# One-hots compared against a row number in PSUM, a ring of five, and a reordered half in a DLRM tower

## The reference

```python
e = jnp.stack([tbl_0[ids[:, 0]], ..., tbl_26[ids[:, 26]]], axis=1)      # 2048 x 27 x 128
inter = jnp.einsum('bfd,bgd->bfg', e, e)                                # pairs f > g are kept: 351
h = jnp.concatenate([bottom, inter_pairs, bottom], axis=1)              # 607
h = jnp.maximum(h @ W_top1 + b_top1, 0.0)                               # 512
h = jnp.maximum(h @ W_top2 + b_top2, 0.0)                               # 256
y = h @ W_top3                                                          # 1
```

## Time and profile before

| | us |
|---|---|
| median of 3 runs (lowest, highest) | 424.97 (424.09, 425.02) |
| the profiled execution | 425.06 |
| its span, first to last instruction | 423.2 |
| busy: PE / PEld | 354.6 / 330.9 |
| busy: POOL / DVE / ACT | 306.2 / 181.0 / 132.9 |

### The profile page before, as it was taken

The page is one execution under the profiler, slowest core; times in us unless marked ns, Lnnn a source line. Parts: engine busy times, 40 slices in busy tenths (PEclk is TensorE's granted clock), DMA queues, the critical chain, the costliest instruction groups (busy, mean ns, idle before and its releaser), DMA issues.

```text
span 423.2 us, 10159 instructions
## 1 busy us (share of the span) xinstructions
PE 354.6 (84%) x4224; PEld 330.9 (78%) x4224; DVE 181.0 (43%) x292; ACT 132.9 (31%) x251; POOL 306.2 (72%) x288
## 2 busy tenths in 40 slices
PE   0094892998999899998999879988999869999937
PEld 0093882998889898988899768987799858988735
DVE  2375845473337522752276133752167232752000
ACT  2222341124322533144313232153221433144303
POOL 6777647787778777877787777877788777877050
PEclk9996895999999999999999989999899989999979
DMA  8958526235432533253333533253332633223020
GB/s 233 224 149 219 144 72 232 61 99 178 103 99 55 176 97 103 49 175 97 74 84 98 166 68 94 53 176 95 76 82 51 208 72 99 49 53 94 16 50 0
DMA packets 46364, 45.74 MB, mean 108 GB/s; under 512 B 34797, under 2 KB 37416, under 8 KB 45296
## 3 DMA queue, kind: packets, MB, share of 16 engines
q1 hardware_dynamic: 34804, 26.09, 22.9%
q0 software_dynamic: 9024, 17.91, 16.4%
q10 hardware_dynamic: 2492, 1.12, 1.1%
HBM read 39.52 MB, written 5.55 MB: 106 GB/s over the span
## 4 chain that ended last, share of the span: by engine, by line
PE 43%; POOL 30%; issue 10%; DMA 8%; SPq 3%; DVE 3%; ACT 2%; ACTq 1%
POOL emb L282 30%; PE work L310 25%; PE work L378 5%; PE gram L338 5%; PE work L321 4%; DMA emb<-in_tbl,ids_all 3%; SPq L233 2%; DMA stages<-in_tbl 2%; DMA h<-in_W_top 1%; PE work L386 1%; PE work L363 1%; DMA h<-in_tbl 1%; DVE tab_lo L429 1%; PE work L365 1%; PE work L364 1%
## 5 line engine op out<-in xcount | busy, mean ns | idle before, releaser
L282 POOL DMA_INDIRECT emb<-in_tbl,ids_all x272 | 299.7, 1102 | 89.4 <-issue 79.3
L310 PE MATMUL work<-onehot,tab_hi 125*128 125x256 f32 x672 | 167.6, 290 | 29.6 <-DVE onehot L441 28.4
L441 DVE TENSOR_SCALAR onehot<-ids_bc,row_idf 125x1024 fp32r<-125x1024 int32 (+1 forms) x208 | 134.4, 663 | 92.3 <-PE work L310 92.0
L310 PE MATMUL work<-onehot,tab_lo 125*128 125x256 f32 x672 | 166.3, 288 | 0.0
L310 PEld LDWEIGHTS work<-onehot,tab_hi 125*128 125x128 f32 x672 | 132.6, 197 | 30.4 <-issue 23.5
L310 PEld LDWEIGHTS work<-onehot,tab_lo 125*128 125x128 f32 x672 | 132.6, 197 | 0.0
L338 PEld LDWEIGHTS gram<-embT 128*54 128x54 f32 x2048 | 55.4, 132 | 19.8 <-issue 12.7
L513 ACT COPY embT<-work 128x512 f32<-128x512 f32 x40 | 29.9, 813 | 126.9 <-PE work L310 126.9
L338 PE MATMUL gram<-embT 128*54 128x52 f32 x2048 | 59.1, 217 | 11.3 <-ACT embT L413 6.0
L321 PE MATMUL work<-ident,emb 128*128 128x128 f32 x272 | 38.8, 283 | 18.3 <-DMA emb<-in_tbl,ids_all 9.8
L321 PEld LDWEIGHTS work<-ident,emb 128*128 128x128 f32 x272 | 30.4, 144 | 24.1 <-issue 11.7
(11 more groups left out here) (31 smaller groups left out, 130.3 us busy)
## 6 DMA issues: line engine op xcount, KB each, us to landing
ids_bc<-in_sel_ids SPq DMA_DIRECT2D x8, 1280.0 KB
grams<-inter SPq DMA_DIRECT2D x64, 84.5 KB
emb<-in_tbl,ids_all POOLq DMA_INDIRECT x272
stages<-in_tbl SPq DMA_DIRECT2D x5, 448.0 KB
h<-in_tbl SPq DMA_DIRECT2D x3, 448.0 KB
stages<-in_tbl SPq DMA_DIRECT2D x2, 560.0 KB
bot<-in_bottom SPq DMA_DIRECT2D x8, 128.0 KB
packed<-grams SPq DMA_DIRECT2D x46, 4.0 KB
```

What stands on the lines that cost most here:

```text
L282: pool.indirect_dma_start(out=emb[:, t % TILE_SLOTS, f, :], out_offset=None, in_=gather_tables[f], in_offset=bass.IndirectOffsetOnAxis(ap= ...
L310: mm = nc.tensor.matmul(out, part[0:k, CHUNK_AT[f] + c, :], onehot[0:k, at % RING, i * HALF:(i + 1) * HALF], start=(c == 0 and i % 2 == 0 ...
L441: nc.vector.tensor_scalar(onehot[0:k, at % RING, 0:len(four) * HALF], ids_bc[0:k, four[0]:four[-1] + 1, :].rearrange("p i n -> p (i n)"), ...
```

## The change

- `BANKS` 4 to 5 and `RING` 3 to 5. To make room, the two staging buffers become `inter` and a new `misc`, and `packed`, `bot` and `y` are parts of `misc`. SP's first load of `bot` and ACT's weight loads wait for the last table's split.
- The one-hot is a tensor against tensor compare; `row_idf`, broadcast along the columns, moves from SBUF to PSUM.
- The first half works in sets of two features (`TWOS`: five sets, 42 one-hots of 512 columns), each set with its own load of ids. ACT rounds the tables of two sets, then those of set j + 2 behind the copies of set j. Later halves keep `FOURS`.
- The even tile's rows go ahead of the last set; in the first half one group goes behind each set from the second on, the last two behind the last. All of them are copied by ACT.
- `mlp1`'s first chunk goes between the last set and the even tile's products. `round_packed` goes behind all four extracts of the even tile.

```diff
-BANKS = 4
+BANKS = 5
-RING = 3
+RING = 5
...
+    TWOS = [(four[a:a + 2], k, chunks) for four, k, chunks in FOURS for a in range(0, len(four), 2)]
+    SETS = [TWOS] + [FOURS] * (HALVES - 1)
...
+    def rows_behind(h, j):
+
+        if h:
+            return range(NGR) if j == max(0, len(FOURS) - 2) else range(0)
+        return range(j - 1, NGR if j == len(TWOS) - 1 else j) if 0 < j <= NGR else range(0)
...
-        row_idf = sb("row_idf", [P, sum(ROW_IDS)])
+        row_idf = ctx.enter_context(nc.psum_tensor("row_idf", [P, sum(ROW_IDS)], F32))
...
-                if n == 0:
-                    sp.dma_start(ids_bc[:, :, :], sel_ids[0].to_broadcast([P, NSEL, HALF])).then_inc(ids_bc_loaded, 16)
+                if i in SET_START:
+                    j = SET_START.index(i)
+                    two = slice(i, i + len(TWOS[j][0]))
+                    sp.dma_start(ids_bc[:, two, :], sel_ids[0][:, two, :].to_broadcast([P, len(TWOS[j][0]), HALF])).then_inc(ids_bc_first[j], 16)
...
+            sp.wait_ge(table_lo, NSEL)
             sp.dma_start(bot[:, :, :], bottom_v[0]).then_inc(bot_loaded, 16)
...
-                for j in range(len(FOURS)):
+                for j in range(len(SETS[h])):
                     select(h, j)
-                rows(2 * h)
+                    rows(2 * h, rows_behind(h, j))
+                if h:
+                    mlp1(h - 1, X_ORDER[:1])
                 products(2 * h, range(GRAMS))
                 if h:
-                    mlp1(h - 1)
+                    mlp1(h - 1, X_ORDER[1:])
...
-                nc.vector.tensor_scalar(onehot[0:k, at % RING, 0:len(four) * HALF],
+                nc.vector.tensor_tensor(onehot[0:k, at % RING, 0:width],
                                         ids_bc[0:k, four[0]:four[-1] + 1, :].rearrange("p i n -> p (i n)"),
-                                        row_idf[0:k, ROW_AT[chunks] + c:ROW_AT[chunks] + c + 1], None, ALU.is_equal).then_inc(onehot_ready, 1)
+                                        row_idf[0:k, ROW_AT[chunks] + c:ROW_AT[chunks] + c + 1].to_broadcast([k, width]), ALU.is_equal).then_inc(onehot_ready, 1)
...
-                for g in range(1, NGR, 2):
-                    rows_out(dve, nc.vector.tensor_copy, 2 * h, g)
...
+                for j in range(len(SETS[h])):
                     select_out(h, j)
-                for g in range(0, NGR, 2):
-                    rows_out(act, nc.scalar.copy, 2 * h, g)
-                extract(2 * h, 0)
+                    if h == 0:
+                        if j + 2 < len(TWOS):
+                            round_tables(j + 2)
+                        elif j + 2 == len(TWOS):
+                            load_weights()
+                    for g in rows_behind(h, j):
+                        rows_out(act, nc.scalar.copy, 2 * h, g)
+                for u in range(GRAMS):
+                    extract(2 * h, u)
                 if h:
                     round_packed(h - 1)
-                for u in range(1, GRAMS):
-                    extract(2 * h, u)
```

More of the change, by code:

```diff
@@ L78, in dlrm_tower @@
     TABLE_ORDER = [i for four, _, _ in FOURS for i in four]
-    ONEHOTS = [(j, c) for j, (_, _, chunks) in enumerate(FOURS) for c in range(chunks)]
+    TWOS = [(four[a:a + 2], k, chunks) for four, k, chunks in FOURS for a in range(0, len(four), 2)]
+    SETS = [TWOS] + [FOURS] * (HALVES - 1)
+    ONEHOTS = [[(j, c) for j, (_, _, chunks) in enumerate(sets) for c in range(chunks)] for sets in SETS]
+    OH_AT = [sum(len(one) for one in ONEHOTS[:h]) for h in range(HALVES + 1)]
     ROW_IDS = sorted({c for _, _, c in FOURS})
     ROW_AT = {c: sum(x for x in ROW_IDS if x < c) for c in ROW_IDS}
-    NOH = len(ONEHOTS)
     GRAMS = P // QUADS // SPAN
@@ L87, in dlrm_tower @@
     COLS = TWO * NG
+    def rows_behind(h, j):
+        if h:
+            return range(NGR) if j == max(0, len(FOURS) - 2) else range(0)
+        return range(j - 1, NGR if j == len(TWOS) - 1 else j) if 0 < j <= NGR else range(0)
+    assert len(TWOS) - 1 <= NGR
+    SET_START = [four[0] for four, _, _ in TWOS]
     use, fill, used, upto = {}, {}, [0] * BANKS, {}
@@ L105, in dlrm_tower @@
     for h in range(HALVES):
-        for j, (four, _, _) in enumerate(FOURS):
+        for j, (four, _, _) in enumerate(SETS[h]):
             for b in range(-(-len(four) // 2)):
                 take("select", h, j, b)
-        for g in range(NGR):
-            take("rows", 2 * h, g)
+            for g in rows_behind(h, j):
+                take("rows", 2 * h, g)
+        upto["gram", 2 * h] = list(used)
         if h:
@@ L142, in dlrm_tower @@
         inter = sb("inter", [P, COLS, QS])
-        stages = sb("stages", [P, 2 * max(CHUNKS) * D])
-        packed = sb("packed", [P, CH, HALF])
-        bot = sb("bot", [P, HALF // P, D])
+        misc = sb("misc", [P, (CH + 2) * HALF])
         x_hi = sb("x_hi", [P, CH + 1, HALF], F32R)
@@ L313, in select, with rows @@
                     mm.then_inc(onehot_used, 1)
-            def rows(t):
-                for g, features in enumerate(GROUPS):
+            def rows(t, groups):
+                for g in groups:
+                    features = GROUPS[g]
                     pe.wait_ge(gathered[t % TILE_SLOTS][g], (t // TILE_SLOTS + 1) * 16 * len(features))
@@ L324, in products @@
             def products(t, us):
-                for b, n in enumerate(upto["rows", t, NGR - 1]):
+                for b, n in enumerate(upto["gram", t]):
                     pe.wait_ge(freed[b], n)
@@ L348, in bottom_rows, with mlp1 @@
                 last.then_inc(filled, 1)
-            def mlp1(h):
+            def mlp1(h, chunks):
                 if h == 0:
                     pe.wait_ge(w1_split, 3)
-                blocks = [take_bank("mlp1", h, m // 2)[:, m % 2 * HALF:(m % 2 + 1) * HALF] for m in range(M1)]
-                for n, c in enumerate(X_ORDER):
-                    k = X_ROWS[c]
+                if X_ORDER[0] in chunks:
+                    for b in range(2):
+                        take_bank("mlp1", h, b)
+                blocks = [bank("mlp1", h, m // 2)[:, m % 2 * HALF:(m % 2 + 1) * HALF] for m in range(M1)]
+                for c in chunks:
+                    k, n = X_ROWS[c], X_ORDER.index(c)
                     if c == CH:
@@ L404, in _ @@
                 products(2 * h + 1, range(2, GRAMS))
-            mlp1(HALVES - 1)
+            mlp1(HALVES - 1, X_ORDER)
             mlp2(HALVES - 1)
@@ L474, in _ @@
             for h in range(HALVES):
-                for n in range(NOH):
-                    if h == 0 and ONEHOTS[n][1] == 0:
-                        for _ in FOURS[ONEHOTS[n][0]][0]:
+                for n, (j, c) in enumerate(ONEHOTS[h]):
+                    if h == 0 and c == 0:
+                        for _ in TWOS[j][0]:
                             split_table(tables)
@@ L494, in _ @@
         def _(act):
[L495 to L505, removed]
+            def round_tables(j):
+                for i in TWOS[j][0]:
+                    n, rows = TABLE_ORDER.index(i), slice(CHUNK_AT[i], CHUNK_AT[i] + CHUNKS[i])
+                    act.wait_ge(table_staged[n % STAGE], 32 * (n // STAGE + 1))
+                    nc.scalar.copy(tab_hi[0:K, rows, :].rearrange("p c d -> p (c d)"), stage[n % STAGE][0:K, 0:CHUNKS[i] * D]).then_inc(table_hi, 1)
@@ new lines, in load_weights @@
+            def load_weights():
+                act.wait_ge(table_lo, NSEL)
+                act.dma_start(w1_bot[0], w_top1[0:D, :]).then_inc(w1_bot_loaded, 16)
+                act.dma_start(w1_bot[1], w_top1[D + PAIRS:, :]).then_inc(w1_bot_loaded, 16)
+                act.dma_start(w2[:, :, :], w_top2.rearrange("(c p) n -> p c n", p=P)).then_inc(weights_loaded, 16)
+                with nc.allow_non_contiguous_dma(reason="a few hundred elements"):
+                    act.dma_start(w3[:, :], w_top3.rearrange("(c p) one -> p (c one)", p=P)).then_inc(weights_loaded, 16)
+                    act.dma_start(b1[:, :], b_top1.rearrange("(c p) -> p c", p=P)).then_inc(weights_loaded, 16)
+                    act.dma_start(b2[:, :], b_top2.rearrange("(c p) -> p c", p=P)).then_inc(weights_loaded, 16)
@@ L507, in select_out @@
             def select_out(h, j):
-                four, k, chunks = FOURS[j]
-                act.wait_ge(onehot_used, h * NOH + max(x for x, one in enumerate(ONEHOTS) if one[0] == j) + 1)
+                four, k, chunks = SETS[h][j]
+                act.wait_ge(onehot_used, OH_AT[h] + max(x for x, one in enumerate(ONEHOTS[h]) if one[0] == j) + 1)
                 for b in range(-(-len(four) // 2)):
```

38 lines of the change are left out of this document (24 added, 14 removed).

## The result

The changed kernel takes 399.74 us (median of 4 runs, 397.87 to 401.33) for 424.53 of the kernel before beside it: ratio 0.9411, 95% interval 0.9367 to 0.9454. The forecast was 399.5 (390 to 412). The profiled execution took 399.54, its span is 397.7.

A forecast was written before the change was run, and what follows sets the result against it. POOL's gathers, stretched beside DVE's one-hots, were taken to bound the kernel from the fourth half on. 67.0 + 307.3 + 23.4 = 397.7 us of span, plus 1.86 around it, gave 399.6, forecast as 399.5 (390 to 412).

The forecast's parts named there:

- start of the second half: Second half's first selection matmul: forecast at 67.0 us for 77.5, 10.5 us earlier, bounds 64 to 77.
- seven halves: Second half's start to the last product: 43.9 us each, 307.3 for 323.2 us, a gain of 15.9.
- tail: Time behind the last product: 22.5 us plus 0.9 because SP's 28 pack loads would end late, 23.4.
- What bounds: POOL's gathers, 1571 ns beside one-hots, bound from the fourth half; at 0.95 to 1.0 us POOL stops being the bound.
- POOL waiting for PE: Expected sign in the new profile that POOL's gathers run ahead of PE; no size given.
- DVE keeps pace: Selection: slower one-hots cost DVE 26.4 us a half for 17.2, yet five buffers leave no PE stall; 0 us taken.
- Order: Reordered work within a half: gains and losses on PE take 43.72 us to 43.9.
- The wait for the roundings: PE, between the even tile's products and mlp1's rest: +1.45 us a half, between +1.2 and +1.8.
- First half: Table splits done at 11.3 us, then DVE bounds; set ends 16.5, 23.8, 31.3, 38.9, 48.5; W1 loads 7.25.
- halves equal within 1 us: Expected sign in the new profile: all seven later halves within 1 us of each other, at 43.9 us.
- clock 1.00: Expected sign in the later halves: PE's clock at 1.00, where a slow half before had 0.97.
- Rival 3: Reordering does better: roundings' wait hidden, second half starts at 64, halves of 42.5, 388 to 391 us; chance 0.11.

The follow-up runs named there:

- early-rounding kernel: The changed kernel with the three ACT roundings of the packed pairs moved from behind the four extracts to just before the last set's copy: 395.41 us, ratio 0.926.

## Why the prediction was right

By its own sum, forecast and measured:

| term | forecast | measured |
|---|---|---|
| start of the second half | 67.0 | 66.1 |
| seven halves | 7 x 43.9 = 307.3 | 309.0 |
| tail | 23.4 | 22.6 |
| span | 397.7 | 397.7 |

The last line is equal to the digit by luck: three small errors cancel, -0.9, +1.7 and -0.8.

- **What bounds.** Right: POOL's share of the bound went with the stretched gathers (1571 to 944 ns), and the run with the old compare brings it back, 419.7 us where 418 was expected. The sign "POOL waiting for PE" hardly showed, 2.1 us in all for 8.5 before: POOL keeps up with PE but does not run ahead.
- **DVE keeps pace.** Right for the five buffers, at 1212 and 679 ns: the 128 matmuls of the wide sets take 15.46 us, 0.12 each, which leaves no room for a wait. The prediction laid the loss of rate to the operand in PSUM; with both operands in SBUF a one-hot took the same (1219 ns), so it comes with the tensor against tensor form. The cushion is thin, as the ring of three shows (2.5 us a half, 1.6 by my sum, which left out the narrow set).
- **Order.** An ordinary half took 43.59 for 43.9. The wait for the roundings, the one term that spoke against the change, was 1.45 by the sum and 1.36 idle (1.4 between halves with and without it, 43.59 and 42.15). It was the change's own loss, and the earlier rounding took it back. One reason given was empty: the transposes behind the second set were to cover DVE, and the run with the rows last shows that five buffers need no such cover. The fifth bank was worth some 0.7 us a half.
- **First half.** DVE's one-hots from 12.32 (11.3 forecast) to 49.68 (48.5), each set's end within 1.6 us of its forecast; the loads of W1 then took 5.6 us instead of 7.25.
- **Tail.** The term of +0.9 was wrong: SP's 28 loads took 10.75 us (11.97 before) and were done 2 us ahead of the last store:

```profile
363.01 10.75 SPq L238 DMA_DIRECT2D misc<-grams  x28
```

- **Left out of the sum** were the drops of the clock in two halves, which cost 2.2 and 1.5 us. In them the signs "halves equal within 1 us" and "clock 1.00" failed; without them the seven halves would have taken 305.3 us, 2.0 less than forecast.
- **Rival 3's time** was mis-added: 64 + 7 x 42.5 + 23.4 + 1.9 is 387, not 388 to 391. The early roundings came near its mechanism, with 42.15 a half.

## What to carry to other kernels

An engine with much idle time can still be the cause, through what its instructions do to a neighbour: look whether the neighbour's instructions are longer while it works, and price the slower form that leaves it alone. Such a form needs a longer ring, and the ring's depth can be worked out from the two pitches and the head start. When a copy or rounding is moved behind others, ask what is queued behind its reader: here the move back was worth 4 us more.

## What the runs showed of the hardware

- GpSimd's indirect DMA issue took 944 ns beside a DVE compare with one SBUF and one PSUM operand, 1571 beside the scalar form (761 ns each), 1970 beside the same compare with both operands in SBUF. DVE's own time hardly depended on the place of the operand (1212, 1219 ns).
- The granted clock fell to its lower level, 1.2 GHz, for 3.4 us in two halves of the changed kernel (PEclk 0.96 above). Both drops came 1 to 2 us behind the end of the 1.36 us wait for the roundings, but the same wait in five other halves was followed by none. The early-rounding kernel does not have this wait, and yet two drops behind its first half: in the half from 65.61, right behind PE's wait of 3.8 us, and in the half from 155.54, 1 us behind a stop of PE of 2.02 us:

```profile
185.46 0.38 PE L388 MATMUL work<-x_hi,w_lo 95*128 95x256 f32 x1 [2.02 <-issue]
```

  So an idle stretch of 1.36 us or more stood ahead of each of these four drops, but not each such stretch brought one. What decides stays open.
- On two chips PE idled with "issue" between the small matmuls of the products, mostly 0.46, 1.16 or 1.86 us at a time (14.9 at most). The halves before the last were 36 to 45 us longer than the last half of the same run, which took what halves took on the first chip. The one program that ran on all three, the kernel before, took 425.34, 697.9 and 691.4 us. On the first chip PE stopped so in its products once, for 1.4 us. No run here tells its cause.
